# A two-pass wavelet block: other channel statistics, and the residual's x loaded by plain transfers and added by VectorE and GpSimd

## What is computed

```
ll, lh, hl, hh = haar_dwt(x)                        # four half-resolution bands, 80 x 80
fused = relu(bn1(conv1x1(concat(ll, lh, hl, hh))))  # 1024 -> 256 channels
sp    = concat(mean over channels(fused), max over channels(fused))
gated = sigmoid(conv7x7(sp)) * fused
ch    = sigmoid(mlp(mean over pixels(gated)) + mlp(max over pixels(gated)))
proj  = relu(bn2(conv1x1(ch * gated)))              # 256 -> 1024 channels
out   = haar_idwt(four quarters of proj) + x        # 160 x 160, 256 channels
```

## Time and profile before

| | us |
|---|---|
| median of 3 runs | 2601.07 (2600.91 to 2601.85) |
| the profiled execution, whole | 2597.0 |
| its span in the trace | 2595.1 |
| TensorE matmul busy | 2469.7 (95%) |
| VectorE busy | 1994.8 (77%) |
| ScalarE busy | 1077.9 (42%) |
| GpSimd busy | 355.2 (14%) |
| HBM read, written | 447.83 MB, 209.92 MB |

### The profile page before, as it was taken

How to read it: one execution, slowest core, us unless ns; L and a number is a source line. 1 busy time by engine, 2 the same in 40 slices (tenths; PEclk the granted TensorE clock), 3 DMA queues, 4 the chain that set the end, 5 groups by cost and what they waited for, 6 DMA issues and landing times. The chain is left out here.

```text
span 2595.1 us, 32968 instructions
## 1 busy us (share of the span) xinstructions
PE 2469.7 (95%) x12996; PEld 2200.7 (85%) x12996; DVE 1994.8 (77%) x2560; ACT 1077.9 (42%) x1413; POOL 355.2 (14%) x346
## 2 busy tenths in 40 slices
PE   4999999999999999999999999999999999987874
PEld 3888889898898989989898988989899898976764
DVE  4656777798778887798777987788877987787875
ACT  2445534354344533354434543345333453334221
POOL 0100111111111111111111111111111111111110
PEclk9999999999999999999999999999999999998897
DMA  3445699999999999999999999999999999898999
GB/s 125 157 147 195 185 267 262 257 297 270 256 270 273 287 261 260 250 304 271 265 266 256 303 263 261 262 280 286 260 259 263 295 268 267 242 248 237 277 272 245
DMA packets 115178, 659.91 MB, mean 254 GB/s; under 512 B 19520, under 2 KB 20560, under 8 KB 115024
## 3 DMA queue, kind: packets, MB, share of 16 engines
q1 hardware_dynamic: 82768, 448.07, 48.8%
q0 software_dynamic: 32256, 209.73, 41.6%
HBM read 447.83 MB, written 209.92 MB: 253 GB/s over the span
## 5 line engine op out<-in xcount | busy, mean ns | idle before, releaser
L375 PE MATMUL pp<-y_hi,wp_hi 128*128 128x480 f32 (+1 forms) x1792 | 674.5, 376 | 59.1 <-DVE y_lo L676 35.8
L615 DVE TENSOR_TENSOR x_lo<-xin,x_hi 128x1920 fp32r<-128x1920 f32 (+1 forms) x224 | 474.0, 2116 | 302.3 <-ACT x_hi L463 302.2
L389 PE MATMUL pf<-x_hi,wf_hi 128*128 128x480 f32 (+1 forms) x1792 | 676.4, 377 | 6.5 <-ACT fused L536 3.5
L375 PE MATMUL pp<-y_lo,wp_hi 128*128 128x480 f32 (+1 forms) x1792 | 670.6, 374 | 0.0
L375 PE MATMUL pp<-y_hi,wp_lo 128*128 128x480 f32 (+1 forms) x1792 | 669.0, 373 | 0.0
L389 PE MATMUL pf<-x_lo,wf_hi 128*128 128x480 f32 (+1 forms) x1792 | 664.5, 371 | 0.0
L389 PE MATMUL pf<-x_hi,wf_lo 128*128 128x480 f32 (+1 forms) x1792 | 664.3, 371 | 0.0
L463 ACT ACTIVATE x_hi<-xin 128x1920 fp32r<-128x1920 f32 (+1 forms) x224 | 418.5, 1869 | 572.1 <-PE pf L389 572.1
L659 DVE SCALAR_TENSOR_TENSOR xout<-sd,both 128x960 f32<-128x960 f32 (+1 forms) x448 | 504.8, 1169 | 49.2 <-DMA out_dram<-xout 41.9
L492 ACT ACTIVATE relu<-pp,t 128x480 f32<-128x480 f32 (+1 forms) x448 | 286.3, 642 | 390.4 <-PE pp L375 349.0
L375 PEld LDWEIGHTS pp<-y_hi,wp_hi 128*128 128x128 f32 x1792 | 341.9, 191 | 110.0 <-DVE y_lo L676 40.6
(11 more groups left out here) (82 smaller groups left out, 1117.2 us busy)
## 6 DMA issues: line engine op xcount, KB each, us to landing
xin<-in_x_dram SPq DMA_DIRECT2D x160, 960.0 KB, 8.3
xout<-in_x_dram POOLq DMA_DIRECT2D x160, 960.0 KB, 10.9
out_dram<-xout SPq DMA_DIRECT2D x160, 960.0 KB, 11.8
xin<-in_x_dram SPq DMA_DIRECT2D x64, 800.0 KB, 7.5
xout<-in_x_dram POOLq DMA_DIRECT2D x64, 800.0 KB, 10.7
out_dram<-xout SPq DMA_DIRECT2D x64, 800.0 KB, 11.0
sigb<-sig_scratch SPq DMA_DIRECT2D x64, 400.0 KB, 8.1
fused<-in_L_conv_fusion_w_dram SPq DMA_DIRECT2D x1, 1024.0 KB, 4.9
```

The costliest lines, as they stand in the source:

```text
L375: mm = pe.matmul(pp[j][:, 0:n_px], w[:, kt, cols], y[:, s.pc, kt, 0:n_px], start=(kt == 0 and m == 0), stop=(kt == CT - 1 and m == 2))
L389: mm = pe.matmul(pf[o][:, 0:n_px].rearrange("p (y w) -> p y w", w=W2), w[:, i, q, o * P:(o + 1) * P], v[:, q % 2, :, q // 2, :], start=(i ...
L615: nc.vector.tensor_tensor(halves(x_lo, i, k), pairs(i, k), halves(x_hi, i, k).bitcast(F32), ALU.subtract).then_inc(xlo_ready[i], 1)
```

## The change

The residual and the channel statistics are both done in other ways, and the lag grows by one slot.

**Residual.** There is no adding DMA. `cells` writes into one buffer `cell` (was: four `xout`). SP loads the residual's x into one of three buffers `xre` by a plain DMA, `residual` adds `cell` to it, the first half of the pixels on VectorE and the second on GpSimd, and SP stores `xre`. `cells` of the next half waits for both additions. GpSimd's addition also waits for `x_lower` of the slot.

**Statistics.** The sum over channels is now a matmul per pixel row with a `pick` matrix that puts the row's sum into its place of an 80 x 80 PSUM area (`add_channels`, behind `fusion(s,1)`). The maximum is no longer transposed on TensorE: VectorE transposes blocks of 32 x 32 within SBUF and reduces them (`turn`), TensorE transposes the result once per image (`across`), VectorE reduces it, and it goes through DRAM into `maps`. The convolution runs one slot later, and `EXTRA` is 7 and `LAG` 21; `GATED` phases are 2 to 5 and LAST is 7.

```
-EXTRA = 6
+EXTRA = 7
...
-        xout = sb("xout", [P, 4, XPM])
+        xre = sb("xre", [P, 3, XPM])
...
+        cell = sb("cell", [P, XPM])
...
+        mx = sd[:, 0, 0:PXM]
+        turned = sd[:, 1, 0:PXM]
...
-        GATED = {1: (0, 1), 2: (2, 3), 3: (4, 5), 4: (6, 7)}
+        GATED = {2: (0, 1), 3: (2, 3), 4: (4, 5), 5: (6, 7)}
...
+        def residual(eng, ops, kc, i, hand, added):
+
+            g = 2 * kc + i
+            n = 2 * px_of(kc)
+            part_of = slice(hand * n, (hand + 1) * n)
+            eng.wait_ge(xre_landed[g % 3], 16 * (g // 3 + 1))
+            eng.wait_ge(cell_ready, 2 * (g + 1))
+            x_part = xre[:, g % 3, part_of]
+            ops.tensor_tensor(x_part, x_part, cell[:, part_of], ALU.add).then_inc(added, 1)
...
+            def load_residual(kc, i):
+
+                g = 2 * kc + i
+                if g == 0:
+                    sp.wait_ge(wf_psum, 4)
+                need(sp, stored[g % 3], 16 * (g // 3))
+                sp.dma_start(xre[:, g % 3, 0:4 * px_of(kc)], dram(x_v, kc, i)).then_inc(xre_landed[g % 3], 16)
...
             def body(s):
+                if s.phase in GATED:
+                    load_sig(s, GATED[s.phase][0])
+                if s.load_second:
+                    load_x(s.k + 2, 0)
+                if s.c and not s.c_is_first:
+                    store(s.kc - 1, 1)
+                if s.c:
+                    load_residual(s.kc, 1)
+                if s.phase in GATED:
+                    load_sig(s, GATED[s.phase][1])
+                if s.load_second:
+                    load_x(s.k + 2, 1)
...
+                if s.c:
+                    store(s.kc, 0)
+                if s.c_next:
+                    load_residual(s.kn, 0)
...
-                nc.gpsimd.dma_start(xout[:, g % 4, 0:4 * px_of(kc)], dram(x_v, kc, i), accum_op=ALU.add
-                                    ).then_inc(x_added[g % 4], 16)
...
+                if s.c and not s.c_is_first:
+                    if s.load_next:
+                        gp.wait_ge(xlo_ready[0], s.k + 2)
+                    residual(gp, nc.gpsimd, s.kc - 1, 1, 1, added_p)
+                if s.turn:
+                    channel_sum(s)
                 if s.c:
...
+                    residual(gp, nc.gpsimd, s.kc, 0, 1, added_p)
...
+                for r in range(ROWS[k % TILES]):
+                    row = FIRST[k % TILES] + r
+                    at, base = row % GROUP, row - row % GROUP
+                    m = min(GROUP, H2 - base)
+                    mm = pe.matmul(sums[base:base + m, :], pick[:, GROUP - 1 - at:GROUP - 1 - at + m],
+                                   sm[:, r * W2:(r + 1) * W2], start=(at == 0), stop=(at == m - 1))
+                mm.then_inc(sum_psum, 1)
...
+                need(dve, added_v, g)
+                need(dve, added_p, g)
+                px = cell[:, 0:4 * n_px].rearrange("p (y w c) -> p y w c", w=W2, c=2)
...
+                nc.vector.transpose(turned[:, 0:blocks * GROUP], mx[:, 0:blocks * GROUP]).then_inc(turned_ready, 1)
+                dve.wait_ge(turned_ready, s.k + 1)
+                need(dve, across_psum, s.b)
+                nc.vector.tensor_reduce(blockmax[:, block:block + blocks],
+                                        turned[:, 0:blocks * GROUP].rearrange("p (n c) -> p n c", c=GROUP),
+                                        AX.X, ALU.max).then_inc(blockmax_ready, 1)
```

More of the change, by code:

```diff
@@ L429, in body @@
-                if s.c:
+                elif s.c:
                     pe.wait_ge(lo_ready, CT * (s.kc + 1))
                     project(s, 0)
-                if s.phase != LAST:
-                    if s.turn:
-                        turn(s)
-                    if s.a:
-                        fusion(s, 1)
+                if s.a:
+                    fusion(s, 1)
+                if s.turn:
+                    add_channels(s)
+                if s.phase == 0:
+                    pe.wait_ge(blockmax_ready, s.k)
+                    for h in range(2):
+                        n = NPX // GROUP // 2
+                        mm = pe.transpose(across[:, h * P:(h + 1) * P], blockmax[:, h * n:(h + 1) * n], ident[:, :])
+                    mm.then_inc(across_psum, 1)
@@ new lines, in body @@
+                if s.phase == 1:
+                    pe.wait_ge(mean_ready, s.nb + 1)
+                    pe.wait_ge(map_landed, 16 * (s.nb + 1))
+                    pe.wait_ge(band_pass, KS * NK)
+                    for j in range(NK):
+                        mm = pe.matmul(conv, band[:, j, :], maps[:, j // KS, j % KS:j % KS + W2],
+                                       start=(j == 0), stop=(j == NK - 1))
+                    mm.then_inc(conv_psum, 1)
+                if s.phase == LAST:
+                    pe.wait_ge(lo_ready, CT * (s.kc + 1))
+                    project(s, 0)
@@ L533, in body @@
                 if s.a:
+                    if s.phase == LAST and s.c:
+                        act.wait_ge(lo_ready, CT * (s.kc + 1))
                     for o in range(CT):
@@ L636, in butterflies @@
                 n_px = px_of(s.kc)
+                if s.a and (i == 1 or s.phase == LAST):
+                    dve.wait_ge(turned_ready, s.k + 1)
+                    dve.wait_ge(blockmax_ready, s.k + 1)
                 for n, j in enumerate((LL, HL)):
@@ L727, in body @@
                     x_lower(s.k + 1, 1)
+                if s.a:
+                    turn(s)
+                if s.phase == 0:
+                    spatial_max(s)
                 if ahead:
@@ L744, in _ @@
                 body(s)
+            residual(dve, nc.vector, NT - 1, 1, 0, added_v)
 _INS = ["x"] + ["L0_conv_" + n for n in (
```

216 lines of the change are left out of this document (109 added, 107 removed).

## The result

| | before | after |
|---|---|---|
| median, us | 2600.99 (2596.39 to 2601.85) | 2650.69 (2649.48 to 2652.01) |
| span of the profiled execution, us | 2595.1 | 2648.6 |
| slot 21 begins, us | 306.2 | 292.6 |
| slot 112 begins, us | 2279.4 | 2318.8 |
| VectorE busy, us | 1994.8 (77%) | 2348.2 (89%) |

The ratio of after to before is 1.0195, with a 95% interval of 1.0177 to 1.0213: slower, by about 2%. 2611 was predicted, in a range of 2552 to 2675. The start became 13.6 us shorter, the middle (slots 21 to 111) 53.0 us longer, the drain 14.1 us longer. So most of the loss is in the stage in which the adding transfers hid before, and the drain, where they had been the bound, gained nothing either.

A forecast was written before the change was run, and what follows sets the result against it. TensorE was taken to bound the middle, adding transfers the drain. Slot 21 at 283.3 plus a middle of 1973.2 - 55 + 59 + 25 = 2002 gave 2285; with 6.7 + 305 + 8, 2605, plus 6: 2611 us, range 2552 to 2675.

The forecast's parts named there:

- the price of `add_channels`: TensorE, slots 21 to 111: six matmuls at 0.14 us, 0.84 for `turn`'s 1.47 per 6-row slot; -55 us.
- The waits: Middle: TensorE waits for `sm` behind a late VectorE, +59 us in gated phases of six images, +25 in phase LAST.
- The start: Slots 0 to 19: 12.5 us per slot becomes 11.9, -12 us; slot 20, without second pass, 10.5 instead of 21.4.
- The drain's ordinary slots: Drain: VectorE takes over as the bound, at 13.8 us per slot and 12.0 for 5 rows.
- the port section: GpSimd and two-SBUF-input VectorE instructions block each other: VectorE's addition behind `sm` loses 1.1 us per slot.
- VectorE's terms: Per 6-row slot: reductions off 1.03 us; two additions 2.3, reduction 0.65, transpose 0.65 on; +2.6 us, and 0.4 for semaphores.
- The port costs nothing: Rival, middle: VectorE's addition gets in before `sm`, so gates cost less or nothing; 2527 to 2595 us, chance 0.32.
- `turn` is dear or meets the port: Rival: VectorE's transpose takes 1.3 us or one-SBUF-input instructions are blocked, 0.65 to 2.25 us per slot; 2627 to 2754, chance 0.15.
- Late transfers: Rival: residual loads on SP's queue wait for stores and hold up loads of x; 2700 us, chance 0.06.
- the forecast's case: Gated slots: VectorE falls behind, `sm` comes late and TensorE waits; ordinary slots fit; 2590 to 2640 us, chance 0.47.

The follow-up runs named there:

- e3: Against before: the new statistics and lag of 21 alone, the residual still by adding DMA into four buffers; 2590.58 us, ratio 0.9969.
- e6: Against after: 24 matmuls of 400 columns, results unread, fill TensorE's wait ahead of `add_channels` in phase LAST; 2636.93 us, ratio 1.0140 to before.
- e5: Against after: in the drain GpSimd begins each half of its addition only when VectorE's gate in front has ended; 2634.75 us, ratio 1.0133 to before.
- e4: Against before: the loaded residual alone, added half by VectorE and half by GpSimd, with old statistics and lag of 20; 2625.72 us, ratio 1.0116.
- e11: New statistics; adding DMAs to chunk 91, then loaded x, GpSimd waiting for drain gates; slot 112's map transfer before the first residual load; 2568.15 us, 0.9885 of before.
- e1: Against after: GpSimd makes the channel sum `sm` ahead of its first addition instead of behind it; 2636.52 us, ratio 1.0157 to before.
- e7: Against after: channel sum first, `add_channels` later in LAST, GpSimd and VectorE's second-block addition there behind `lower`, GpSimd waiting for drain gates; 2613.46 us, 1.0054 of before.

## Why the prediction was right in sign and range, and short in size

The forecast was 10 us over the median of before, the result 50. The span was to be 2605 and was 2648.6, so 43.6 us have to be found (the profiled span also stood 2 us under the median here and not 6, which takes 4 off again).

| | predicted | measured | missing |
|---|---|---|---|
| slot 21 begins | 283.3 | 292.6 | +9.3 |
| middle | 2002 | 2026.2 | +24.2 |
| drain | 320 | 329.8 | +10 |

- **The middle: the price of `add_channels` was the mis-sized term.** It was to take 0.84 us in place of `turn`'s 1.47, and an ordinary slot to come down from 22.5 to 21.9 us. It came down by less than 0.4, to 22.14, so `add_channels` costs 1.1 us. The cheapest way to price the whole term is e3, whose middle is 1959.5 us; less its waits (10.5 + 4.3, and 0.5 of smaller ones) and half of its 6.8 us at the lower clock, 1941 us are left, which is 32 us under 1973.2, not 55. This makes 23 of the 24 us. The lines at 689.39 to 690.96 show where the price was short. The six matmuls take 0.94 us (689.70 to 690.64) and not 0.84. And the steps at both ends, 0.31 us into `add_channels` and 0.32 behind the first matmul of `project`, are each 0.1 us longer than the 0.22 between two matmuls of one kind, which a price per matmul leaves out. That is 1.13 us in all. `turn` had one such step, behind it. What in the engine makes the step is open.
- **The waits: right in sum by luck, wrong in make-up.** 59 + 25 = 84 us were predicted for gates and phase LAST. What 2026.2 leaves over 1941 is 85 us. But TensorE's waits are only 61 of them; the other 24 are the clock at its lower level behind the waits (64.9 us, so 32 us of lost pace, part of it inside the waits). The prediction had no term for the clock, and its waits were 23 us too long. The gates' waits are 31.5 us and not 59: `x_lower` of half 0 starts 1.9, 4.1 and 5.2 us behind `x_hi` in phases 3, 4 and 5, less than the 2.9 us more per slot of the sum. Phase LAST's waits are 28.4 us in six slots, 4.7 each and not 3.6: its `x_lower` was taken to start 7.4 us into the slot as in an ordinary one, and starts up to 10.6 us into it, behind the two additions. With the slow stretches each slot of phase LAST is 7.6 us longer than an ordinary one. e6 shows the clock's share there; in phase 5 it is read from the rows only.
- **The start.** A slot of 11.9 us was predicted; with `sm` waited for 17 times (11.7 us) it takes 12.1, and the convolution's slot 14.1. Slots 0 to 19 gained 2.3 us (241.9 to 239.6) where 12 were predicted. Slot 20 went from 21.4 to 11.2 us (10.5 predicted). Here the link from x_lo over `sm` to `add_channels` was taken at 0.4 us per slot and was up to 1.5.
- **The drain's ordinary slots: right.** 13.8 us predicted, 13.5 measured, with VectorE the bound (busy for 301.58 of 329.8 us) and a DMA share of 0.71. What was missing is a block: the port section counted VectorE's additions and `lower`, and left out the gate, which reads two SBUF operands as well. Eight gates took 3 us, +14.0 us by e5. The other miss is slot 113 with its wait for the map, 20.1 us instead of 13.8. The two make 20 us and the drain was only 10 short: ordinary slots that were 0.3 us shorter than forecast gave some 7 back, and the rest isn't traced.
- **VectorE's terms: right.** Reduction 0.65 as predicted, transpose 0.67 (0.65), the addition 1.15 (1.16) unblocked and up to 2.13 blocked; GpSimd's addition 2.27 (2.25).

**The rivals.** *The port costs nothing* is out: 1.45 us in the mean instead of 1.15, and e5. *`turn` is dear or meets the port* is out: 0.67 us beside GpSimd's addition. That transpose begins before the addition; the reduction, which begins while the addition runs, takes 0.65 us, as without one. By these rows an instruction with one SBUF input isn't blocked. The Trainium skill ("SBUF — State Buffer", § Who interferes with whom) has this as a rule, and the trace agrees. The rows of before could have said so too, against what the prediction writes: their butterflies take one operand from PSUM and one from SBUF, and ran on beside `sm`. *Late transfers* is out: no wait of TensorE or VectorE for x, and a load of x for the first pass in 4.5 us as before, one for the residual in 6.6. The mechanism of the forecast's case held in the gated slots: VectorE late behind gates, and `sm` late behind VectorE. In phase LAST VectorE is late by what it has to do in that slot, with two additions among it.

**What the residual costs**, by experiment and not by the sum: 28 us alone (e4), and some 59 on top of the new statistics (after against e3: 1.0195 - 0.9969 = 0.0226 of 2600). The statistics alone are the change's good half.

## What to carry to other kernels

Work that is moved off a DMA queue onto an engine is only free in the stages where that engine isn't the late one: price each stage by itself, and keep the old way where it wins (e11 is 1.1% under before, after 2.0% over). Two halves of a change that lean on the same slack must be priced together, not one at a time (-7 and +28 made +50). And an idle gap of TensorE costs more than its length: add the slow stretch behind it, and list every instruction with two SBUF operands that a long GpSimd instruction can meet.

## What the runs showed of the hardware that I had not expected

- Behind an idle gap of 5 us TensorE's clock was at its lower level for most of the next 6.9 us (0.59 in the mean), and matmuls without a use put into the gap made the kernel 13.8 us faster. Kernels with shorter waits show less of it, if not in strict order: 64.9 us at the lower level in after's middle (longest wait 5.1 us), 27.3 in e1's (4.2), 34.1 in e4's (3.5), 17.1 in e7's (2.9), 6.8 in e3's (2.2).
- A block lasts as long as the other engine's instruction: a gate of 0.98 us took 3.01 beside a GpSimd addition of 960 elements, and 5.03 beside one of 1920. It also hits the custom reduction that the gate is, not only plain additions. A reduction with one SBUF input, begun while such an addition of 960 ran, took its usual 0.65 us.
- GpSimd's addition, begun 0.16 us behind a gate, itself took 2.91 us instead of 2.27, which fits a wait for the gate's end: both sides lose.
